# A spiking recurrent layer and a mixture of experts on one core: the recurrent state carried step by step inside the neuron loop, and both gates made by one comparison and one product

## The reference, cut to what matters

```
def lif_step(v, x_t):
    v = v + (x_t - v) * 0.5
    s = (v - 1.0 >= 0)
    return v * (1 - s), s
# attention part, over t:
vr, r = lif_step(vr, R[t]); vk, k = lif_step(vk, K[t]); vv, v = lif_step(vv, V[t])
h = h * 0.9 + k * v
y[t] = r * h
x1 = layernorm(x + y @ Wo.T)
s1 = lif(x1 @ W1.T + b1);  s2 = lif(s1 @ W2.T + b2)
a  = layernorm(x1 + s2);   x3 = layernorm(x + a)
# mixture of experts
gates = softmax(x3 @ Wg + bg); g, i = top_k(gates, 2); g = g / sum(g)
out = layernorm(x3 + sum_j g[j] * (x3 @ We[i[j]] + be[i[j]]))
```

## Time and profile before

| | |
|---|---|
| median of 3 runs | 1075.88 us (1075.11 to 1075.92) |
| the profiled execution | 1075.18 us, of which its span is 1073.4 us |
| DVE busy | 979.2 us, 91% of the span |
| PE busy | 964.1 us, 90% |
| POOL, ACT busy | 602.5 us (56%), 547.8 us (51%) |

### The profile page before, as it was taken

The page is one execution under the profiler, slowest core; times in us unless marked ns, Lnnn a source line. Parts: engine busy times, 40 slices in busy tenths (PEclk is TensorE's granted clock), DMA queues, the critical chain, the costliest instruction groups (busy, mean ns, idle before and its releaser), DMA issues.

```text
span 1073.4 us, 21899 instructions
## 1 busy us (share of the span) xinstructions
PE 964.1 (90%) x7552; PEld 930.0 (87%) x7552; DVE 979.2 (91%) x3273; ACT 547.8 (51%) x1270; POOL 602.5 (56%) x726
## 2 busy tenths in 40 slices
PE   5776669999999999999999999999999999988892
PEld 5666669999999999999999999999999999888882
DVE  6898988999999999999999999999999999999862
ACT  4333334455555565555555555555555665454453
POOL 1011121667766666666776666667776666564452
PEclk8788889999999999999999999999999999899997
DMA  4210112444444545444543454544444344446574
GB/s 160 89 50 30 40 40 50 86 94 98 98 86 86 106 99 109 99 100 89 107 91 83 95 109 99 108 100 99 90 99 91 85 101 93 95 90 129 118 134 92
DMA packets 53967, 99.82 MB, mean 93 GB/s; under 512 B 5984, under 2 KB 5984, under 8 KB 53856
## 3 DMA queue, kind: packets, MB, share of 16 engines
q0 software_dynamic: 32256, 58.73, 31.9%
q1 hardware_dynamic: 16992, 31.30, 9.2%
q10 hardware_dynamic: 4608, 8.39, 2.1%
HBM read 31.29 MB, written 8.39 MB: 37 GB/s over the span
## 4 chain that ended last, share of the span: by engine, by line
DVE 48%; PE 42%; issue 5%; ACT 4%; DMA 1%; POOL 0%; DVEq 0%; POOLq 0%; ACTq 0%
PE ps_e L341 18%; DVE U L710 10%; PE ps_proj L411 10%; DVE V L717 8%; PE ps_proj L417 5%; DVE hidden L763 4%; DVE stats L775 4%; DVE hidden L752 4%; DVE y L768 2%; PE ps_proj L341 2%; DVE z L734 2%; PE ps_attn L377 2%; PE ps_proj L396 2%; DVE x1n L802 2%; DVE y L748 2%
## 5 line engine op out<-in xcount | busy, mean ns | idle before, releaser
L341 PE MATMUL ps_e<-we_hi,x_hi 128*128 128x256 f32 (+1 forms) x1024 | 293.6, 287 | 5.6 <-ACT odd_sum L583 5.6
L341 PE MATMUL ps_e<-we_hi,x_lo 128*128 128x256 f32 (+1 forms) x1024 | 287.8, 281 | 0.0
L341 PE MATMUL ps_e<-we_lo,x_hi 128*128 128x256 f32 (+1 forms) x1024 | 287.7, 281 | 0.0
L710 DVE SCALAR_TENSOR_TENSOR U<-V,U 128x256 f32<-128x256 f32 (+5 forms) x656 | 257.5, 403 | 7.1
L717 DVE SCALAR_TENSOR_TENSOR V<-U 128x256 f32<-128x256 f32 (+5 forms) x656 | 228.7, 359 | 1.0
L546 ACT ACTIVATE U<-ps_proj,cst 128x256 f32<-128x256 f32 x320 | 135.3, 480 | 167.0 <-PE ps_proj L417 84.4
L1091 POOL TENSOR_SCALAR veps<-mv 128x2 f32<-128x2 f32 x128 | 47.5, 371 | 299.2 <-DVE mv L781 299.2
L1105 POOL TENSOR_SCALAR s<-U 128x256 fp32r<-128x256 f32 x208 | 214.6, 1057 | 1.2 <-DVE V L717 1.2
L341 PEld LDWEIGHTS ps_e<-we_hi,x_hi 128*128 128x128 f32 x1024 | 193.5, 189 | 6.3 <-ACT odd_sum L583 6.2
L341 PEld LDWEIGHTS ps_e<-we_hi,x_lo 128*128 128x128 f32 x1024 | 193.8, 189 | 0.1
L341 PEld LDWEIGHTS ps_e<-we_lo,x_hi 128*128 128x128 f32 x1024 | 193.0, 188 | 0.0
(11 more groups left out here) (88 smaller groups left out, 2194.5 us busy)
## 6 DMA issues: line engine op xcount, KB each, us to landing
acc<-term POOLq DMA_DIRECT2D x96, 256.0 KB, 3.7
odd_sum<-term POOLq DMA_DIRECT2D x96, 256.0 KB, 3.3
xt<-x_T SPq DMA_DIRECT2D x33, 256.0 KB, 3.0
xa<-x_tok SPq DMA_DIRECT2D x32, 256.0 KB, 3.3
xb<-cst SPq DMA_DIRECT2D x32, 256.0 KB, 2.3
xb<-x_tok POOLq DMA_DIRECT2D x32, 256.0 KB, 6.0
out<-res ACTq DMA_DIRECT2D x32, 256.0 KB, 2.1
term<-w SPq DMA_DIRECT2D x8, 256.0 KB, 5.3
```

Of the source, the lines that this page charges most:

```text
L341: mm = pe.matmul(dst, lhs, rhs, start=(i == 0), stop=(i == n - 1))
L710: v.scalar_tensor_tensor(out=U[:, s, t, c0:c1], in0=V[:, c0:c1], scalar=0.5, in1=U[:, s, t, c0:c1], op0=ALU.mult, op1=ALU.add).then_inc(do ...
```

## The change

The scan goes. `hidden` and `decay` are replaced by two tiles `kv` and `h` with the time outermost. The state steps of chunk k are issued inside the LIF loop of beat k itself: in batches of four time steps, each a comparison of v, a comparison of k with the product, both over 4 steps by 32 columns, and then four instructions of 32 columns, h[t] = 0.9 h[t - 1] + kv[t]. Batches 0 to 2 take one instruction for each of the slots 7 to 12, 15 to 20 and 23 to 28; the two comparisons of batch 3 go into slots 30 and 31, and its four steps of h into the four first places of `y_stage` in the next beat (slots 0 to 3 of a steady beat, slot -1 elsewhere). The last place of `y_stage` makes y from h as before. In every slot the state step comes ahead of what `side` issues besides. The four instructions of L880 become a comparison of both experts' numbers for both tiles at once (`chosen`) and one product; the comparison has a slot of its own, 10 in a steady beat.

```diff
-STEADY = ... gate=(6, 7, 8, 9, 12, 13, 14, 14, 15, 16, 18, 20), ...
+STEADY = ... gate=(6, 7, 8, 9, 10, 12, 13, 14, 15, 16, 18, 20), ...
...
-        decay = sb("decay", [P, DK * B, STEPS])
-        hidden = sb("hidden", [P, 2, DK * B, STEPS])
+        kv = sb("kv", [P, STEPS, DK * B])
+        h = sb("h", [P, STEPS, DK * B])
...
-        Y_STEPS, ..., GATE_STEPS, ... = 6, ..., 17, ...
+        Y_STEPS, ..., GATE_STEPS, ... = 2, ..., 15, ...
...
+            def state_step(b, n):
+                batch, part = divmod(n, 2 + BATCH)
+                steps = slice(BATCH * batch, BATCH * (batch + 1))
+                if some(b.value(STATE_STEPS, 0, n)):
+                    dve.wait_ge(state_steps, b.value(STATE_STEPS, 0, n))
+                if part == 0:
+                    last = 2 * STEPS * b.k + 2 * (BATCH * (batch + 1) - 1) + 1
+                    dve.wait_ge(lif, last)
+                    if b.halves:
+                        dve.wait_ge(lif_half, last)
+                    op = v.tensor_scalar(kv[:, steps, :], U[:, b.k % 2, steps, 2 * DK * B:3 * DK * B],
+                                         THRESHOLD, None, ALU.is_ge)
+                elif part == 1:
+                    op = v.scalar_tensor_tensor(out=kv[:, steps, :], in0=U[:, b.k % 2, steps, DK * B:2 * DK * B],
+                                                scalar=THRESHOLD, in1=kv[:, steps, :],
+                                                op0=ALU.is_ge, op1=ALU.mult)
+                else:
+                    t = BATCH * batch + part - 2
...
+                    op = v.scalar_tensor_tensor(out=h[:, t, :], in0=h[:, (t - 1) % STEPS, :], scalar=DECAY,
+                                                in1=kv[:, t, :], op0=ALU.mult, op1=ALU.add)
+                op.then_inc(state_steps, 1)
...
+            def state_in_lif(b, slot):
+                if not 0 <= b.k < CHUNKS:
+                    return
+                batch, part = divmod(slot - 7, 2 * BATCH)
+                if slot in (2 * STEPS - 2, 2 * STEPS - 1):
+                    state_step(b, STATE_STEPS - STATE_TAIL - 2 + slot - (2 * STEPS - 2))
+                elif slot >= 7 and batch < STEPS // BATCH - 1 and part < 2 + BATCH:
+                    state_step(b, (2 + BATCH) * batch + part)
...
             def y_stage(b, step):
...
+                if step < STATE_TAIL:
+                    state_step(Beat(b.k - LAG_Y), STATE_STEPS - STATE_TAIL + step)
+                    return
+                after(state_steps, STATE_STEPS, LAG_Y, b, STATE_STEPS)
...
+                for k in range(DK):
+                    v.scalar_tensor_tensor(out=y[:, k * N:(k + 1) * N].rearrange("p (t b) -> p t b", b=B),
+                                           in0=spikes_view((b.k - 1) % 2, k, 1), scalar=THRESHOLD,
+                                           in1=h[:, :, k * B:(k + 1) * B],
                                            op0=ALU.is_ge, op1=ALU.mult).then_inc(y_steps, 1)
...
                 if step == 4:
+                    chain(6)
+                    both = lambda tile: tile[:].rearrange("p j k -> p (j k)").unsqueeze(2).to_broadcast([P, 2 * TILES, E])
+                    v.tensor_tensor(chosen[:].rearrange("p j k e -> p (j k) e"),
+                                    cst[:, C_IOTA:C_IOTA + E].unsqueeze(1).to_broadcast([P, 2 * TILES, E]),
+                                    both(top_atf), ALU.is_equal).then_inc(gate_steps, 1)
...
-                if step in (7, 8):
-                    for j in range(TILES):
-                        v.tensor_scalar(dst[:, j, :], cst[:, C_IOTA:C_IOTA + E], top_atf[:, j, at:at + 1],
-                                        weight[:, j:j + 1], ALU.is_equal, ALU.mult).then_inc(gate_steps, 1)
+                if step == 8:
+                    chain(11)
...
+                    v.tensor_tensor(chosen_rows, chosen_rows, both(gweight), ALU.mult).then_inc(gate_steps, 1)
                 if step == 9:
...
+                    v.tensor_tensor(gate[:, gslot], chosen[:, :, 0, :], chosen[:, :, 1, :],
+                                    ALU.add).then_inc(gate_steps, 1)
```

More of the change, by code:

```diff
@@ L41 @@
 DECAY = 0.9
+BATCH = 4
+STATE_STEPS = STEPS + 2 * STEPS // BATCH
+STATE_TAIL = BATCH
 COL_H1 = RKV_TILES * B
@@ L216, in build @@
         gdiff, gexp = sb("gdiff", [P, TILES]), sb("gexp", [P, TILES])
-        gden, g1st, g2nd = sb("gden", [P, TILES]), sb("g1st", [P, TILES]), sb("g2nd", [P, TILES])
-        gate_b = sb("gate_b", [P, TILES, E])
+        gden, gweight = sb("gden", [P, TILES]), sb("gweight", [P, TILES, 2])
+        chosen = sb("chosen", [P, TILES, 2, E])
         gate = sb("gate", [P, 2, TILES, E])
@@ L737, in z_sum @@
                                        op0=ALU.is_ge, op1=ALU.add).then_inc(z_ready, 1)
-            def y_stage(b, step):
[L741 to L753, removed]
-                                           op0=ALU.is_ge, op1=ALU.mult).then_inc(y_steps, 1)
[L755 to L771, removed]
@@ new lines, in state_step @@
+            def state_step(b, n):
[16 more added lines that the diff above has]
+                    t = BATCH * batch + part - 2
+                    if t == 0 and some(b.value(Y_STEPS, LAG_Y, Y_STEPS)):
+                        dve.wait_ge(y_steps, b.value(Y_STEPS, LAG_Y, Y_STEPS))
+                    op = v.scalar_tensor_tensor(out=h[:, t, :], in0=h[:, (t - 1) % STEPS, :], scalar=DECAY,
+                                                in1=kv[:, t, :], op0=ALU.mult, op1=ALU.add)
+                op.then_inc(state_steps, 1)
@@ new lines, in state_in_lif @@
+            def state_in_lif(b, slot):
[6 more added lines that the diff above has]
+                    state_step(b, (2 + BATCH) * batch + part)
+            def y_stage(b, step):
+                if step < STATE_TAIL:
+                    state_step(Beat(b.k - LAG_Y), STATE_STEPS - STATE_TAIL + step)
+                    return
+                after(state_steps, STATE_STEPS, LAG_Y, b, STATE_STEPS)
+                if some(b.value(1, LAG_Y)):
+                    dve.wait_ge(attn_done, b.value(1, LAG_Y))
+                for k in range(DK):
+                    v.scalar_tensor_tensor(out=y[:, k * N:(k + 1) * N].rearrange("p (t b) -> p t b", b=B),
+                                           in0=spikes_view((b.k - 1) % 2, k, 1), scalar=THRESHOLD,
+                                           in1=h[:, :, k * B:(k + 1) * B],
+                                           op0=ALU.is_ge, op1=ALU.mult).then_inc(y_steps, 1)
@@ L860, in gate_stage @@
                 if step == 4:
+                    chain(6)
[3 more added lines that the diff above has]
+                                    both(top_atf), ALU.is_equal).then_inc(gate_steps, 1)
+                if step == 5:
                     dve.wait_ge(gexp_ready, b.value(1, LAG_M, 1))
@@ L863, in gate_stage @@
                     v.tensor_scalar(gden[:], gexp[:], 1.0, None, ALU.add).then_inc(gate_steps, 1)
-                if step == 5:
-                    chain(8)
-                    v.reciprocal(g1st[:], gden[:]).then_inc(gate_steps, 1)
                 if step == 6:
                     chain(9)
-                    v.tensor_tensor(g2nd[:], gexp[:], g1st[:], ALU.mult).then_inc(gate_steps, 1)
-                if step in (7, 8):
+                    v.reciprocal(gweight[:, :, 0], gden[:]).then_inc(gate_steps, 1)
@@ L871, in gate_stage @@
+                if step == 7:
                     chain(10)
[L872 to L878, removed]
-                    for j in range(TILES):
-                        v.tensor_scalar(dst[:, j, :], cst[:, C_IOTA:C_IOTA + E], top_atf[:, j, at:at + 1],
-                                        weight[:, j:j + 1], ALU.is_equal, ALU.mult).then_inc(gate_steps, 1)
@@ L882, in gate_stage @@
-                if step == 9:
-                    chain(14)
-                    v.tensor_tensor(gate[:, gslot], gate[:, gslot], gate_b[:], ALU.add).then_inc(gate_steps, 1)
+                    v.tensor_tensor(gweight[:, :, 1], gexp[:], gweight[:, :, 0], ALU.mult).then_inc(gate_steps, 1)
+                if step == 8:
+                    chain(11)
+                    both = lambda tile: tile[:].rearrange("p j k -> p (j k)").unsqueeze(2).to_broadcast([P, 2 * TILES, E])
+                    chosen_rows = chosen[:].rearrange("p j k e -> p (j k) e")
+                    v.tensor_tensor(chosen_rows, chosen_rows, both(gweight), ALU.mult).then_inc(gate_steps, 1)
@@ L885, in gate_stage @@
+                if step == 9:
+                    chain(12)
+                    if some(b.value(E - 1, LAG_M + 2, E - 1)):
+                        dve.wait_ge(term_ready, b.value(E - 1, LAG_M + 2, E - 1))
+                    v.tensor_tensor(gate[:, gslot], chosen[:, :, 0, :], chosen[:, :, 1, :],
+                                    ALU.add).then_inc(gate_steps, 1)
                 if step == 10:
@@ L945, in side @@
                 split_weights(b, slot)
+                state_in_lif(b, slot)
```

(6 more changed lines are left out.)

12 lines of the change are left out of this document (6 added, 6 removed).

## The result

The changed kernel takes 1058.88 us (median of 4 runs, 1056.95 to 1059.57) against 1075.9 us (4 runs, 1075.11 to 1077.01): ratio 0.9835, 95% interval 0.9821 to 0.9848. The forecast was 1061 us, 1048 to 1080. The same kernel on another occasion gave 1059.12 us, ratio 0.9863 (0.9848 to 0.9878). The profiled execution took 1059.16 us with a span of 1057.4 us.

A forecast was written before the change was run, and what follows sets the result against it. It took the hand-over between DVE and PE, both about 90% busy, to bound. Steady beats -10, fill -3 and drain -2 us took 1075.18 to 1060.2; with 0.7 for the median, 1061 us, range 1048 to 1080.

The forecast's parts named there:

- The loop: Steady beat: PE from transposes to attn, attn, DVE from ln1_sum to transposes, added small instructions; 29.55 us instead of 29.95.
- the 0.60 us: What the state steps in slots 8 to 12 add to DVE's stretch from ln1_sum to the transposes.
- the new wait: DVE at ln1_sum in a steady beat would wait for attn on PE, some 0.9 us.
- The price of a small instruction: On DVE, a 32-column instruction costs 0.10 us from start to start, not its whole duration.
- The rival that had them cost their duration: DVE's small instructions cost their whole durations, its loop is 31.2 us and bounds; about 1115 us, chance 0.10.
- The covers: In steady beats y is done near 522.8 against 524.39 when PE wants it, and x1_lo isn't later.
- DVE's own loop: DVE's work in a steady beat: 29.95 less 3.0 in slots 0 to 4 plus 1.7 added, 28.65 us.
- The port: Rival: state steps and products of slots 0 to 4 wait half a POOL instruction each; 1085 us, chance 0.08.
- the stand against x_lo: The first membrane's 1.30 us beside POOL's x_lo stays, within the 4.2 us taken for slots 0 to 4.
- Fill: Beats 0 to 6: beats 1 to 6 gain, beat 0 loses 2 us; -3 us, within -8 and +3.
- Drain: Last beats: the gate pairs of L880 lie on the path in some four beats, 0.5 to 0.6 each; -2 us.
- the edges: Fill and drain outside the 25 steady periods: -3 and -2 us.

The follow-up runs named there:

- x3: Changed kernel with no state step in slots 7 to 12 of a steady beat, the 18 instructions moved to slots 15 to 29: 1043.46 us, ratio 0.9703.
- x4: Changed kernel with the four state steps in slots 9 to 12 of a steady beat issued twice, into a spare tile: 1067.28 us, ratio 0.991.
- x2: Changed kernel with the old gates (four small instructions in slots 14 and 15, no comparison in slot 10): 1071.63 us, ratio 0.9952.
- x6: x3 with four state steps in slots 22 to 24 issued twice, the second time into a spare tile: 1069.51 us, ratio 0.9942.
- x5: Changed kernel with the four state steps in slots 25 to 28 of a steady beat issued twice, into a spare tile: 1060.28 us, ratio 0.9856.
- x8: x6 with GpSimd's x_lo in two instructions of 256 columns instead of one of 512: 1073.09 us, ratio 0.9992.
- x9: x3 with GpSimd's x_lo in two halves: 1043.67 us, ratio 0.9705.

## Why the prediction was right

**The loop.** The prediction added up 21.23 + 2.03 + 5.59 + 0.70 = 29.55 us. The profile after has 461.28 - 440.06 = 21.22, then 463.21 - 461.28 = 1.93, then 469.52 - 463.21 = 6.31 for 6.29: 29.46. x3 and x4 show the last term from both sides: without the 0.60 us the beat is 0.61 shorter, with 0.40 more it is 0.39 longer. The mechanism that the prediction named (y off the path, a wait on DVE at `ln1_sum` in its place) is what the profile shows, and the new wait is 0.61 us for the 0.9 reckoned.

**The price of a small instruction.** 0.10 from start to start at a duration of 0.18 or 0.19, as drawn from the earlier trace rows; x4 shows that it is what the path pays. The rival that had them cost their duration is out. The Trainium skill ("VectorE: DVE Perf Modes", The DRAIN you can't avoid) says that the next instruction doesn't start until the pipe is empty, and adds that one which isn't held starts earlier. The trace shows the second case: the next one starts at 0.10 of 0.18 us.

**The covers.** y is 1.6 us early, as reckoned. x1_lo isn't later, as forecast, but it keeps only 0.13 us to spare, and x2 shows how much hangs on that: without the gates' 0.7 us the state change brings nothing in the steady beats. DVE's own loop was put at 28.65 and is 29.46 - 0.61 = 28.85.

**The port.** This rival didn't come about, though there is a small effect of its kind. The h steps of slots 1 and 3 take 0.39 us beside GpSimd's spikes instead of 0.18, 0.2 more on two of four and not 0.5 on each. What the prediction misplaced is the stand against x_lo: it left 1.30 us in the first membrane, and now reset 15 stands in slot 31 (1.15), so slots 0 to 4 take 459.60 - 455.98 = 3.6 us and not 4.2, while the end of the beat grows. The sum hardly moves, since both lie outside of the path.

**Fill and drain.** That the sum came within some 2 us of the median is partly luck: three terms were off and made up for each other. Fill: -3 forecast, -0.15 and -1.85 in the two pairs of profiles, -2.4 between the means; single executions of it scatter by more than the term. Drain: -2 forecast, -0.8 and 0.0 in the two pairs. Beats 31 and 32 were counted as steady, which gave them -0.8 together, and they bring -4.1 and -3.5 us in the two pairs. So the 25 periods of beats 7 to 32 gave -15.1 and -12.4 for the -10 forecast, and the edges -0.9 and -1.8 for -5. In beat 31, which has no `rkv` any more, PE waited 3.30 us for y before; the windows of the kernel before show the granted clock (PEclk) ahead of that pause, in its first part, and over its end with most of `attn`, which starts at 914.37:

```profile
core 0: us, PE busy (x) PEld busy (x) DVE busy (x) ACT busy (x) POOL busy (x), PEclk, DMA share, GB/s
904.00:911.00 7.00, 7.00 (x61) 6.85 (x59) 6.10 (x13) 5.57 (x14) 5.96 (x7) 1.00 0.22 40
911.00:913.00 2.00, 0.06 (x1) 0.00 (x0) 2.00 (x3) 0.22 (x1) 2.00 (x3) 1.00 0.34 131
913.50:917.50 4.00, 3.13 (x7) 2.52 (x8) 3.41 (x9) 0.00 (x0) 4.00 (x6) 0.50 0.00 0
```

The clock fell from 2.4 GHz to 1.2 within the pause, and `attn` took 3.78 us instead of 1.99 (3.11 in the second profile of this kernel). After the change PE waits 1.11 us there and `attn` takes 1.99 (901.80). An earlier y is worth its own pause and, where the pause was long, the slow matmuls behind it.

## What to carry to other kernels

When two engines are both 90% busy, neither total says what an edit is worth. Write the loop that closes over one period, term by term, and price an edit only where it lies on it; keep beside it the slack of each wait that is next. Two halves of a change can each bring nothing in the steady beat and together half a microsecond, so an edit that measures as nothing alone may be what another one needs. And place new small instructions where an engine waits or where another engine carries the path: the same instructions outside of slots 7 to 12 were worth nearly as much again as the change itself (some 15 us beside 17).

## What the runs showed of the hardware

GpSimd's x_lo, a tensor-tensor instruction on two tensors in SBUF, holds DVE instructions that meet it until it has ended, however small they are: a state step of 32 columns took 1.73 us instead of 0.18 (x6), a comparison of 128 columns 1.13 and 1.23 instead of 0.22 (x3, x5), reset 15 1.15 instead of 0.41 (the changed kernel). Not every one is held: the subtraction that makes x3_lo, which reads one of its operands from PSUM, took 0.68 us beside it (454.09 in the changed kernel), as it does elsewhere.

The Trainium skill ("SBUF — State Buffer", on the shared port pair) has the lock for the length of one instruction. Between two such instructions both was seen. In x8 a state step that started 0.05 us ahead of the two halves was held for both (1.87 us against 1.76). In x9 a comparison that started 0.35 us into the first half ended 0.08 us after it, while the second ran. What decides is not shown: the two DVE instructions differ in kind and in when they start.

Beside GpSimd's one-input spikes (0.93 us each) a two-input state step took at most 0.39 us instead of 0.18, 0.2 more, where by the lock for a whole instruction it could have been 0.9.

Part of what slots 0 to 4 gained may be layout and not the scan. With the time innermost (64 bytes from one element to the next) the two instructions of y took 0.69 us each, and with it outermost 0.50 on average, on the same number of columns. The product of 512 columns took 1.27 us, and the four products of 128 that replace it 0.28 each. No run changes the layout alone.
